# Expert tiles: remainders of at most 64 rows share a tile in pairs

## The chip, the cores and the metric

The kernel runs on one core of a Trainium2 chip. The metric is the device time in microseconds of one execution, the median of several runs. Engines are named as in the profile: PE (TensorE; PEld its weight loads), DVE (VectorE), ACT (ScalarE), POOL (GpSimd), SP (SyncE, whose queue the profile calls SPq).

## The reference, cut to what matters

2048 tokens (16 x 128) of 256 channels pass an attention-like step made of causal convolutions, and then a mixture of 16 experts with 4 choices a token, beside a shared expert.

```python
x = x + xattn(layernorm(x), k, bias, ctx, ctx)     # convolutions by head, products, sums over 8
xt = layernorm(x).reshape(-1, 256)                 # 2048 tokens
scores = softmax(xt @ Wg.T)                        # 16 experts in 4 groups
# the two best groups, in them the four best experts; their scores are the weights
h = silu(xt @ W1[e].T) * (xt @ W3[e].T)            # 176 wide, for each expert e
y = sum over the 4 choices of weight * (h @ W2[e].T)
z = silu(xt @ Ws1.T) * (xt @ Ws3.T) @ Ws2.T        # shared, 352 wide
x = x + y + z
```

## The kernel before, in words

The tokens are 16 units of 128. A first stage runs unit by unit: the convolutions as products with Toeplitz matrices, VectorE's products, and `sums` (line 1111), which adds them up by products with a 128x32 matrix whose outputs go to 32 partitions each, at 0, 32, 64 and 96 of one bank. From unit 6 on routing runs beside it on VectorE, four units at a time (`less_max` to `slots`).

GpSimd scatters each normalised row four times into `rows_scratch`, a region for each expert (line 563), together with its weights and its place in the output. The rows of an expert stand there in the order of the units. All experts' weights, 352 + 176 KB for each, are loaded once and stay in SBUF (`load_expert`, lines 263 to 269).

Then the shared expert runs on TensorE: `up_shared` (twelve steps), with `down_shared` for the unit outputs between. VectorE multiplies (`hidden_shared`), adds (`add_z`) and in between makes the tile lists: `tile_starts`, `tile_places`, `tile_owners`, `tile_ends` work on 128x256 arrays (a partition for each tile, an element for each unit and expert) and find each tile's expert, its first row and how many units it must wait for. TensorE turns these columns into rows in `tile_lists` (line 1217), in its order right behind step 9 of `up_shared`, with a wait on `owners_ready`. `last_sends` works out how many sends each read-back must await. `tile_map` writes the lists and signals `map_ready`; then SyncE gathers the first tiles.

The routed stage runs over 79 tiles of 128 rows (80, of which the last can't be needed), ordered by the unit in which a tile's first row lies. An expert with a remainder has one tile that is partly padding; tiles past the last real one work on padding. For each tile, in `routed_step` of each engine:
- SyncE: `gather` (lines 310 to 318) reads the tile's number from SBUF, waits until the tile four before was turned and taken, and starts a load of 144 KB.
- TensorE: `up` (line 1189), two products of 352 columns, then `turn_x` of the next tile (line 1208), `down` of the tile two before (line 1251), `turn_h` (line 1199). A float32 product shows as two records.
- ScalarE: silu, a copy of the turned rows, a copy of the output. VectorE: `take` (the two gate columns, line 955, behind a load of the expert's number), `hidden`, `copy_h`, `place` (the row numbers).
- GpSimd: `send`, an indirect DMA that writes 128 output rows to `y_scratch` (line 617).

When all tiles with rows of a pair of units have been sent, SyncE reads their 4 x 256 outputs back (`read_back`, 1 MB, after four loads of counts from SBUF, lines 322 to 328), VectorE adds them in four steps (`add_part`) and SyncE stores the units (`store`, line 332). In each turn of eight tiles one read-back and one store stand between the gathers; the last two units are read back one by one between the last gathers.

SyncE works in order: what waits in its queue holds all gathers behind it. The order on every engine is written out by hand; `routed` runs the first eight tiles unrolled, the others in a loop of four.

## Time and profile before

| | us |
|---|---|
| median of three runs | 414.01 (413.64 to 414.26) |
| the profiled execution | 410.32 |
| its span, first to last instruction | 408.6 |
| TensorE busy | 395.1 |
| VectorE, ScalarE, GpSimd busy | 241.7, 168.0, 185.1 |
| DMA, mean over the span | 195 GB/s |

The profile is of one execution. Busy times are sums over the span; matmuls are pipelined, so the record of one (its latency) is longer than its distance to the next, and distances between starts are what counts. The first stage ends at about 135 us, the shared expert's products run until 205, between them and the routed tiles at first; the first tile's up product is at 199.66. In a timeline a row gives the start, the length, the engine, the line, the operation with output and inputs, and how many instructions were put together.

### The profile page before, as it was taken

The numbers are of one execution on the slowest core, as the hardware profiler recorded it, in microseconds if no ns is written. First come the engines' busy times: TensorE is split into PE (matmuls) and PEld (weight loads), VectorE is DVE, ScalarE is ACT, GpSimd is POOL, SyncE is SP. The second block draws the span as 40 slices with busy tenths as digits, with TensorE's granted clock in tenths as the row PEclk, the third lists the DMA queues.
The fourth block names the chain that finished last, engine by engine and source line by source line (L and its number), as shares of the span: only waits on it lengthen the run. The fifth ranks groups of instructions, "written<-read, shape, count | busy, mean of one in ns | idle before, by whom it ended". The sixth has DMA issues, their size and how long they took to land.

```text
span 408.6 us, 9369 instructions
## 1 busy us (share of the span) xinstructions
PE 395.1 (97%) x2144; PEld 292.9 (72%) x2145; DVE 241.7 (59%) x663; ACT 168.0 (41%) x513; POOL 185.1 (45%) x231
## 2 busy tenths in 40 slices
PE   7999999999999999999999999999999999999994
PEld 6788788788888445555877777777676767677772
DVE  3576577898978447674344444464646464646464
ACT  5348557555653640111234334333343433333341
POOL 3253333338887644646463333333333333333344
PEclk9999999999999999999999999999999999999999
DMA  7964664468869996454443333646364645454662
GB/s 238 368 232 144 204 223 143 144 243 295 283 222 379 322 315 203 147 217 154 141 148 117 110 110 109 200 134 211 124 213 134 201 146 189 158 192 154 219 222 98
DMA packets 39421, 79.71 MB, mean 195 GB/s; under 512 B 5792, under 2 KB 26624, under 8 KB 37344
## 3 DMA queue, kind: packets, MB, share of 16 engines
q1 hardware_dynamic: 32528, 59.57, 44.5%
q0 software_dynamic: 6864, 19.80, 12.5%
q8 instruction: 12, 0.20, 0.2%
q14 instruction: 17, 0.14, 0.1%
HBM read 54.95 MB, written 24.40 MB: 194 GB/s over the span
## 4 chain that ended last, share of the span: by engine, by line
PE 69%; DVE 8%; DMA 7%; SPq 5%; issue 5%; POOL 3%; ACT 1%; DVEq 1%; POOLq 0%
PE heads L1189 17%; PE bank L1251 13%; PE heads L1097 9%; PE heads L1229 8%; PE bank L1241 5%; DMA toep<-rows_scratch 4%; PE heads L1099 4%; PE bank L1208 4%; DVE kv L636 3%; PE heads L1199 3%; PE bank L1111 3%; SPq L324 2%; DVE prod L665 2%; POOL rows_scratch L563 2%; DMA toep<-toep_in 2%
## 5 line engine op out<-in xcount | busy, mean ns | idle before, releaser
L617 POOL DMA_INDIRECT y_scratch<-toep,dest_i x79 | 76.6, 969 | 119.0 <-DVE dest_i L962 106.0
L1189 PE MATMUL heads<-w,toep 128*128 x316 | 106.6, 460 | 0.0
L1251 PE MATMUL bank<-w,toep 88*128 x316 | 82.0, 381 | 0.5 <-DVE toep L932 0.5
L563 POOL DMA_INDIRECT rows_scratch<-rows,slot_i x64 | 63.4, 991 | 38.9 <-issue 19.1
L1097 PE MATMUL heads<-toep,kv 128*128 128x256 f32 x256 | 77.8, 386 | 2.4 <-DVE kv L636 1.7
L1189 PEld LDWEIGHTS heads<-w,toep 128*128 128x128 f32 x316 | 53.8, 190 | 17.0
L458 ACT ACTIVATE toep<-heads 128x176 f32<-128x176 f32 x79 | 25.0, 317 | 82.9 <-PE heads L1189 82.9
L1251 PEld LDWEIGHTS bank<-w,toep 88*128 88x128 f32 x316 | 53.7, 190 | 6.1 <-issue 1.2
L932 DVE COPY toep<-heads 88x256 f32<-88x256 f32 x79 | 33.2, 421 | 37.9 <-PE heads L1199 37.8
L1099 PEld LDWEIGHTS heads<-toep,kv 128*128 128x128 f32 x256 | 48.6, 190 | 6.6
L665 DVE TENSOR_TENSOR prod<-heads,ctx_rep 128x1024 f32<-128x1024 f32 x32 | 39.0, 1219 | 22.2 <-PE bank L1111 19.8
L1099 PE MATMUL heads<-toep,kv 128*128 128x128 f32 x256 | 49.2, 274 | 0.0
L925 DVE SCALAR_TENSOR_TENSOR toep<-toep,heads 128x176 f32<-128x176 f32 x79 | 31.4, 397 | 27.4 <-ACT toep L458 24.6
L464 ACT ACTIVATE toep<-bank 128x256 f32<-128x256 f32 x79 | 30.3, 383 | 41.5 <-PE bank L1251 41.5
L1229 PE MATMUL heads<-xn_tr_all,ws 128*128 128x512 f32 (+1 forms) x96 | 43.1, 595 | 0.0
L1097 PEld LDWEIGHTS heads<-toep,kv 128*128 128x128 f32 x256 | 38.8, 192 | 3.2 <-DVE kv L636 1.8
L1208 PEld LDWEIGHTS bank<-ident,toep 128*128 128x128 f32 x158 | 21.9, 141 | 23.6 <-issue 11.0
L636 DVE TENSOR_TENSOR kv<-bank,ctx_tr 128x2048 f32<-128x2048 f32 x15 | 34.2, 2281 | 0.1
L452 ACT ACTIVATE toep<-bank 128x256 f32<-128x256 f32 x79 | 30.2, 382 | 5.7 <-PE bank L1208 5.6
L1208 PE MATMUL bank<-ident,toep 128*128 128x128 f32 x158 | 30.4, 274 | 1.6 <-DMA toep<-rows_scratch 1.6
L1229 PEld LDWEIGHTS heads<-xn_tr_all,ws 128*128 128x128 f32 (+1 forms) x96 | 16.9, 181 | 19.6 <-issue 19.3
L955 DVE COPY toep<-toep 128x2 f32 x79 | 14.0, 177 | 28.1 <-issue 22.3
(158 smaller groups left out, 439.8 us busy)
## 6 DMA issues: line engine op xcount, KB each, us to landing
ctx_rep<-ctxr_in SPq DMA_DIRECT2D x16, 1024.0 KB, 4.9
toep<-rows_scratch SPq DMA_DIRECT2D x79, 144.0 KB
prod<-y_scratch SPq DMA_DIRECT2D x7, 1024.0 KB, 5.2
w<-w_in SPq DMA_DIRECT2D x16, 352.0 KB
w<-w_in SPq DMA_DIRECT2D x16, 176.0 KB
rows_scratch<-pad_row SPq DMA_DIRECT2D x17, 144.0 KB
ctx_tr<-ctxt_in SPq DMA_DIRECT2D x16, 128.0 KB, 5.0
toep<-toep_in SPq DMA_DIRECT2D x4, 512.0 KB, 7.1
```

Of the source, the lines that this page charges most:

```text
L563: pool.indirect_dma_start(rows_d, bass.IndirectOffsetOnAxis(ap=slot_i[:, u, k:k + 1].bitcast(U32), axis=0), rows[:, u, :], None).then_inc( ...
L617: pool.indirect_dma_start(y_d, bass.IndirectOffsetOnAxis(ap=dest_i[b][:, 0:1].bitcast(U32), axis=0), y_sb[b], None).then_inc(y_sent[b], 16)
L636: nc.vector.tensor_tensor(kv[:, u % 2, :, :].rearrange("p b (g i j) -> p (b g) i j", i=C, j=C), tr_ps.rearrange("p b (g i) -> p (b g) i", ...
L665: nc.vector.tensor_tensor(prod[:, par, :, :], y_ps[par], ctx_rep[:, u % 2, par::2, :], ALU.mult).then_inc(prod_ready, 1)
L925: nc.vector.scalar_tensor_tensor(hid[p], act1[p], picked[:, b, 0:1], up_ps[p][:, INTER:], ALU.mult, ALU.mult).then_inc(hid_ready, 1)
L932: nc.vector.tensor_copy(hid_tr[p], ht_ps[p]).then_inc(htr_ready, 1)
L1097: nc.tensor.matmul(y_ps[par][:, i, :], kv[:, q, 0, h * P:(h + 1) * P], toep[:, q * HH + h, :], start=True, stop=False)
L1099: last = nc.tensor.matmul(y_ps[par][:, i, P:], kv[:, q, 1, h * P:(h + 1) * P], toep[:, q * HH + h, 0:P], start=False, stop=True)
L1189: last = nc.tensor.matmul(up_ps[p], x_tr[p][:, blk, :], w13[:, bass.ds(e, 1), blk, :].rearrange("p a n -> p (a n)"), start=blk == 0, stop= ...
L1208: last = nc.tensor.transpose(xt_ps[p][:, blk, :], src[:, blk * P:(blk + 1) * P], ident[:])
L1229: last = nc.tensor.matmul(bank[2 * (s % 2) + w][0:rows_c, :].rearrange("p (u n) -> p u n", u=GT), ws13[:, blk, w, c0:c0 + rows_c], xn_tr_a ...
L1251: last = nc.tensor.matmul(dn_ps[p], hid_tr[p][:, c, :], w2[:, bass.ds(e, 1), c, :].rearrange("p a n -> p (a n)"), start=c == 0, stop=c == 1)
```

## The change

The remainder of an expert that has at most 64 rows no longer gets a tile of its own. Such remainders are paired: two experts' share a tile, one in the rows 0 to 63, one in 64 to 127. There are 72 tiles, 64 + 8, and all are run. The tiles 16 to 23 are the mixed ones: they are gathered in two halves, their up and down products are two for each block, 64 columns of the stationary side each, into the partitions 0 to 63 and 64 to 127. The weights for the upper half are not indexed in SBUF: each mixed tile has its own 352 + 176 KB loaded from memory again (`load_other`), into buffers that are free by then, one pair of loads behind each of the gathers 8 to 15. Where fewer than eight pairs exist, a mixed tile works for one expert in both halves.

VectorE's lists grow by the columns for the second halves. `hidden_shared(5)`, `(8)` and `(9)` stand elsewhere among them. In the loop SyncE's four count loads of a read-back are put behind one gather each, the read-back and the store come together behind the fourth gather, and begin one turn later; the last four read-backs (two pairs and two single units) stand behind the last gather.

```diff
-TILES = TOK * TOPK // P + E
+TILES = TOK * TOPK // P + E // 2
+MIXED0, MIXED = 16, E // 2
+HALF = P // 2
...
-LIVE = TILES - 1
+LIVE = TILES
...
+        other_w13 = [mem[:, 0:W13].rearrange("p (b n) -> p b n", b=LB) for mem in other_mem]
+        other_w2 = [mem[0:HI, W13:W13 + W2].rearrange("p (c n) -> p c n", c=2) for mem in other_mem]
...
+            with eng.Fori(until // DEPTH, LIVE // DEPTH - 1) as it:
...
-                sp.dma_start(xg[b], rows_d[bass.ds(at, P)]).then_inc(rows_in[b], 16)
+                if is_mixed(t):
+                    sp.dma_start(xg[b][0:HALF], rows_d[bass.ds(at, HALF)]).then_inc(rows_in[b], 16)
+                    also = sp.value_load(other_row[0:1, t - MIXED0:t - MIXED0 + 1], min_val=0, max_val=E * REGION + HALF)
+                    sp.dma_start(xg[b][HALF:P], rows_d[bass.ds(also, HALF)]).then_inc(others_in[b], 16)
+                else:
+                    sp.dma_start(xg[b], rows_d[bass.ds(at, P)]).then_inc(rows_in[b], 16)
+            def load_other(g):
+                if g < 4:
+                    sp.wait_ge(s_up, GROUPS * len(CHUNKS))
+                elif g < 7:
+                    sp.wait_ge(s_down, UNITS)
+                e = sp.value_load(other_e[0:1, g:g + 1], min_val=0, max_val=E - 1)
+                sp.dma_start(other_w13[g].rearrange("p b n -> p (b n)"),
+                             w13_d[:, bass.ds(e, 1), :, :].rearrange("p a b n -> p (a b n)")).then_inc(other_in[g], 16)
+                sp.dma_start(other_w2[g].rearrange("p c n -> p (c n)"),
+                             w2_d[:, bass.ds(e, 1), :, :].rearrange("p a b n -> p (a b n)")).then_inc(other_in[g], 16)
...
+            for g in range(MIXED):
+                gathers(1, g, g + 1)
+                load_other(g)
+            gathers(2, 0, 8)
+            gathers(3, 0, 8)
+            for b in range(DEPTH):
+                gathers(4, b, b + 1)
             read_back(0, 0, 2, back, back_in)
-            gathers(3, 3, 8)
-            with sp.Fori(4, 9) as m:
-                gathers(m, 0, 2)
-                store(m - 4, m * 2 - 8, 2)
-                gathers(m, 2, 3)
-                read_back(m - 3, m * 2 - 6, 2, back, back_in)
-                gathers(m, 3, 8)
-            gathers(9, 0, 2)
-            store(5, 10, 2)
-            gathers(9, 2, 3)
-            read_back(6, 12, 2, back, back_in)
-            gathers(9, 3, 5)
-            read_back(7, 14, 1, back_last[0], last_in[0])
-            gathers(9, 5, 7)
-            read_back(8, 15, 1, back_last[1], last_in[1])
-            store(6, 12, 2)
-            store(7, 14, 1)
-            store(8, 15, 1)
+            gathers(4, 4, 8)
+            with sp.Fori(5, 9) as m:
+                sends = []
+                for b in range(DEPTH):
+                    gathers(m, b, b + 1)
+                    sends.append(sends_of(m - 4, b))
+                store(m - 5, m * 2 - 10, 2)
+                read_back(m - 4, m * 2 - 8, 2, back, back_in, sends)
+                gathers(m, 4, 8)
+            for i in range(4):
+                read_back(5 + i, SPANS[5 + i][0], SPANS[5 + i][1], back_last[i], last_in[i])
+                if i == 0:
+                    store(4, 8, 2)
+            for i in range(4):
+                store(5 + i, SPANS[5 + i][0], SPANS[5 + i][1])
...
+                all_rows = upto[:, :, UNITS - 1:UNITS].to_broadcast([P, E, UNITS])
+                then(nc.vector.scalar_tensor_tensor(short, first, -1.0 * HALF, all_rows, ALU.add, ALU.is_ge))
+                then(nc.vector.tensor_tensor(alone, in_units(short), starts, ALU.mult))
+                then(nc.vector.tensor_tensor(starts, starts, alone, ALU.subtract))
...
+                nc.vector.tensor_tensor_scan(one_row(place_of), go_on[:, 1:2].to_broadcast([P, UE]), one_row(starts), -1.0,
+                                             ALU.mult, ALU.add)
+                then(nc.vector.tensor_tensor_scan(one_row(alone_of), go_on[:, 1:2].to_broadcast([P, UE]), one_row(alone), 0.0,
+                                                  ALU.mult, ALU.add))
+            def mixed_places():
+                then(nc.vector.tensor_scalar(enough, io_2e[:], alone_of[:, UNITS - 1, E - 1:E], None, ALU.is_lt))
+                then(nc.vector.tensor_reduce(blocks_of, enough, AX_X, ALU.add))
+                nc.vector.tensor_scalar(mixed, io_p[:], MIXED0 - 0.5, None, ALU.is_gt)
+                then(nc.vector.scalar_tensor_tensor(late, io_p[:], -1.0 * MIXED0, blocks_of, ALU.add, ALU.is_ge))
+                nc.vector.scalar_tensor_tensor(mine, late, blocks_of, io_p[:], ALU.mult, ALU.subtract)
+                then(nc.vector.tensor_tensor(mixed, mixed, late, ALU.subtract))
+                then(nc.vector.scalar_tensor_tensor(mine, mixed, 1024.0, mine, ALU.mult, ALU.subtract))
+                then(nc.vector.tensor_scalar(sole, io_p[:], 2.0, 1.0 - 2 * MIXED0, ALU.mult, ALU.add))
+                then(nc.vector.tensor_scalar(own[7], sole, 1.0, None, ALU.add))
...
+                then(nc.vector.scalar_tensor_tensor(owns, place_of, mine, starts, ALU.is_equal, ALU.mult))
+                nc.vector.scalar_tensor_tensor(t0, alone_of, sole, alone, ALU.is_equal, ALU.mult)
+                then(nc.vector.scalar_tensor_tensor(t1, alone_of, own[7], alone, ALU.is_equal, ALU.mult))
+                nc.vector.tensor_reduce(own[2], one_row(t1), AX_X, ALU.add)
+                nc.vector.tensor_tensor(owns_other, owns, t1, ALU.add)
+                then(nc.vector.tensor_tensor(owns, owns, t0, ALU.add))
+                every = io_e[:].unsqueeze(1).to_broadcast([P, UNITS, E])
+                for i, who in enumerate((owns, owns_other)):
+                    nc.vector.tensor_tensor(t0 if i == 0 else t2, who, every, ALU.mult)
+                    last = nc.vector.scalar_tensor_tensor(t1 if i == 0 else t3, in_units(first), -1.0 * (P + E * REGION), who,
+                                                          ALU.add, ALU.mult)
+                    then(last)
+                nc.vector.tensor_reduce(own[0], one_row(t0), AX_X, ALU.add)
+                nc.vector.tensor_reduce(own[1], one_row(t1), AX_X, ALU.add)
+                nc.vector.tensor_reduce(own[3], one_row(t2), AX_X, ALU.add)
+                nc.vector.tensor_reduce(own[4], one_row(t3), AX_X, ALU.add)
+                nc.vector.tensor_reduce(own[5], one_row(owns), AX_X, ALU.add)
+                then(nc.vector.tensor_reduce(own[6], one_row(owns_other), AX_X, ALU.add))
...
+            def tile_lists_of():
+                past_full = float(TOK * TOPK // P)
+                then(nc.vector.tensor_scalar(dead_e, io_p[:], past_full - 0.5, None, ALU.is_gt))
+                nc.vector.tensor_scalar(own[7], io_p[:], past_full + E - 1, None, ALU.subtract)
+                nc.vector.tensor_scalar(lists[0], own[5], -1.0, 1.0, ALU.mult, ALU.add)
+                then(nc.vector.tensor_scalar(lists[3], own[6], -1.0, 1.0, ALU.mult, ALU.add))
+                then(nc.vector.tensor_tensor(dead_e, dead_e, own[7], ALU.mult))
+                then(nc.vector.tensor_scalar(dead_e, dead_e, E - 1.0, None, ALU.add))
+                nc.vector.scalar_tensor_tensor(lists[0], lists[0], dead_e, own[0], ALU.mult, ALU.add)
+                nc.vector.scalar_tensor_tensor(lists[3], lists[3], dead_e, own[3], ALU.mult, ALU.add)
+                nc.vector.scalar_tensor_tensor(lists[1], own[0], float(REGION), own[1], ALU.mult, ALU.add)
+                nc.vector.scalar_tensor_tensor(lists[4], own[3], float(REGION), own[4], ALU.mult, ALU.add)
                 nc.vector.tensor_scalar(of_expert, io_e[:], own[0], None, ALU.is_equal)
-                nc.vector.scalar_tensor_tensor(own[3], own[2], 0.0, own[0], ALU.max, ALU.add)
-                nc.vector.tensor_scalar(own[6], own[1], float(P + E * REGION), None, ALU.add)
-                then(nc.vector.scalar_tensor_tensor(own[4], own[0], float(REGION), own[1], ALU.mult, ALU.add))
+                nc.vector.tensor_scalar(own[7], own[2], -1.0 * HALF, float(HALF), ALU.mult, ALU.add)
+                then(nc.vector.tensor_scalar(own[6], own[1], float(P + E * REGION), None, ALU.add))
...
+                then(nc.vector.tensor_tensor(lists[4], lists[4], own[7], ALU.add))
...
+                    nc.vector.tensor_copy(full_to[:, at:at + 1], place_of[0:1, u0 + units - 1, E - 1:E])
+                    last = nc.vector.tensor_copy(alone_to[:, at:at + 1], alone_of[0:1, u0 + units - 1, E - 1:E])
                 then(last)
+                then(nc.vector.tensor_scalar(past, full_to, MIXED0 - 0.5, None, ALU.is_gt))
+                then(nc.vector.scalar_tensor_tensor(need, past, blocks_of[0:1], full_to, ALU.mult, ALU.add))
+                then(nc.vector.tensor_scalar(past, alone_to, 0.5, None, ALU.is_gt))
+                then(nc.vector.tensor_scalar(alone_to, blocks_of[0:1].to_broadcast([1, len(SPANS)]), MIXED0 - 1.0, None, ALU.add))
+                then(nc.vector.tensor_tensor(past, past, alone_to, ALU.mult))
+                then(nc.vector.tensor_tensor(need, need, past, ALU.max))
...
+                if is_mixed(t):
+                    dve.wait_ge(others_in[b], (t - MIXED0) // DEPTH * 16 + 16)
+                    nc.vector.tensor_copy(picked[0:HALF, b, :].unsqueeze(2), gates[0:HALF, :, bass.ds(e, 1)])
+                    e = dve.value_load(other_e[0:1, t - MIXED0:t - MIXED0 + 1], min_val=0, max_val=E - 1)
+                    nc.vector.tensor_copy(picked[HALF:P, b, :].unsqueeze(2), gates[HALF:P, :, bass.ds(e, 1)]).then_inc(taken, 1)
+                else:
+                    nc.vector.tensor_copy(picked[:, b, :].unsqueeze(2), gates[:, :, bass.ds(e, 1)]).then_inc(taken, 1)
...
             marks(3)
+            hidden_shared(5)
             places(3)
-            hidden_shared(5)
...
             tile_places()
+            mixed_places()
+            hidden_shared(8)
             tile_owners()
-            hidden_shared(8)
+            tile_lists_of()
             tile_ends()
+            hidden_shared(9)
             last_sends()
-            hidden_shared(9)
             tile_map()
...
+            for m in range(4):
                 steps(m, 0, 8)
-            steps(3, 0, 8, 0, 0)
-            with dve.Fori(4, 9) as m:
-                steps(m, 0, 8, m - 3, m * 2 - 6)
-            steps(9, 0, 6, 6, 12)
-            add_last(0, (0, 1))
-            steps(9, 6, 7)
-            add_last(0, (2, 3))
+            with dve.Fori(4, 8) as m:
+                steps(m, 0, 8, m - 4, m * 2 - 8)
+            steps(8, 0, 8, 4, 8)
             copy_h(LIVE - 1, (LIVE - 1) % 2)
-            add_last(1, range(TOPK))
+            for i in range(4):
+                add_last(i)
...
+                if is_mixed(t):
+                    g = t - MIXED0
+                    pe.wait_ge(other_in[g], 32)
+                    for blk in range(LB):
+                        nc.tensor.matmul(up_ps[p][0:HALF], x_tr[p][:, blk, 0:HALF],
+                                         w13[:, bass.ds(e, 1), blk, :].rearrange("p a n -> p (a n)"),
+                                         start=blk == 0, stop=blk == LB - 1)
+                        last = nc.tensor.matmul(up_ps[p][HALF:P], x_tr[p][:, blk, HALF:P], other_w13[g][:, blk, :],
+                                                start=blk == 0, stop=blk == LB - 1)
+                    last.then_inc(up_done, 1)
+                    return
...
+                for i in range(5):
+                    last = nc.tensor.transpose(map_ps[i], tmp[0:TILES, 8 + i:9 + i], ident[0:TILES, 0:TILES])
...
+                if is_mixed(t):
+                    for c in range(2):
+                        nc.tensor.matmul(dn_ps[p][0:HALF], hid_tr[p][:, c, 0:HALF],
+                                         w2[:, bass.ds(e, 1), c, :].rearrange("p a n -> p (a n)"),
+                                         start=c == 0, stop=c == 1)
+                        last = nc.tensor.matmul(dn_ps[p][HALF:P], hid_tr[p][:, c, HALF:P], other_w2[t - MIXED0][:, c, :],
+                                                start=c == 0, stop=c == 1)
+                    last.then_inc(dn_done, 1)
+                    return
...
```

## Rows read from the trace of the kernel before

**Rows 1.** The page, busy time of the engines over the span.

```profile
PE 395.1 (97%) x2144; PEld 292.9 (72%) x2145; DVE 241.7 (59%) x663; ACT 168.0 (41%) x513; POOL 185.1 (45%) x231
```

**Rows 2.** Chain that ended last, 185 to 408 us: by line; start, length, what.

```profile
by line: PE heads L1189 31.5%; PE bank L1251 24.1%; DMA toep<-rows_scratch 8.1%; PE bank L1208 6.7%; PE heads L1199 6.1%; PE bank L1241 4.7%; issue 4.4%; SPq L324 3.6%; PE heads L1229 3.1%; SPq L314 2.3%; SPq L318 1.1%; SPq L328 0.8%; DVEq 
...
392.16 0.87 PE bank L1251 x4
393.25 1.19 PE heads L1189 x4
```

**Rows 3.** Timeline of TensorE, routed stage: start, length, engine, line, operation.

```profile
205.28 1.35 PE L1189 MATMUL heads<-w,toep 128*128 x4
...
207.77 1.35 PE L1189 MATMUL heads<-w,toep 128*128 x4
...
398.06 1.35 PE L1189 MATMUL heads<-w,toep 128*128 x4
```

**Rows 4.** Chain that ended last, 272 to 290 us, around a read-back.

```profile
280.71 0.38 SPq L328
...
282.35 4.60 DMA toep<-rows_scratch
```

**Rows 5.** Timeline of TensorE, around the sums of one unit.

```profile
18.38 0.38 PE L1099 MATMUL heads<-toep,kv 128*128 128x128 f32 x2
18.70 1.07 PE L1111 MATMUL bank<-prod,sum_i 128*32 128x256 f32 x16
19.70 0.70 PE L1122 MATMUL bank<-vc,skip_w 128*128 128x256 f32 x2
20.23 0.38 PE L1077 MATMUL bank<-ident,v 128*128 128x128 f32 x2
```

**Rows 6.** Timeline of VectorE and TensorE, 175 to 190 us.

```profile
178.20 0.68 DVE L838 TENSOR_TENSOR_SCAN kv<-go_on,kv 128x256 f32<-128x256 f32 x1
...
181.06 0.15 DVE L850 SCALAR_TENSOR_TENSOR route_tmp<-io_p,kv 128x1 f32<-128x1 f32 x1
...
184.12 0.15 DVE L864 TENSOR_SCALAR route_tmp<-route_tmp 128x1 f32<-128x1 f32 x1
...
184.53 0.37 PE L1217 MATMUL bank<-ident,route_tmp 80*1 80x80 f32 x3
```

**Rows 7.** Start of TensorE; windows of the end: length, busy, clock, DMA, GB/s.

```profile
1.87 4.95 PE L1160 MATMUL heads<-ident 128*128 128x128 f32 x22 [1.87 <-POOL ident L521]
...
7.40 1.28 PE L1163 MATMUL heads<-ident 128*128 128x128 f32 x10
...
406.40:407.40 1.00, 0.00 (x0) 0.70 0.32 131
```

**Rows 8.** SyncE issuing expert weights; a window of the same stretch.

```profile
128.59 0.35 SPq L265 DMA_DIRECT2D w<-w_in  x1
...
129.91 0.35 SPq L265 DMA_DIRECT2D w<-w_in  x1
...
125.00:130.00 5.00, 4.53 (x40) 3.52 (x38) 3.31 (x7) 2.41 (x9) 4.17 (x5) 1.00 1.03 363
```

**Rows 9.** Last issues; a send; DMA landings (count, KB, median us); last addition.

```profile
389.84 1.49 SPq L318 DMA_DIRECT2D toep<-rows_scratch  x2
...
394.18 0.35 SPq L328 DMA_DIRECT2D ctx_rep<-y_scratch  x1
...
396.77 0.96 POOL L617 DMA_INDIRECT y_scratch<-toep,dest_i  x1 [1.33 <-DVE dest_i L962]
...
y_scratch<-toep,dest_i POOLq DMA_INDIRECT x79, 2.4
...
ctx_rep<-y_scratch SPq DMA_DIRECT2D x2, 512.0 KB, 3.6
...
out<-resid SPq DMA_DIRECT2D x2, 128.0 KB, 1.7
...
403.30 0.42 DVE L1037 TENSOR_TENSOR resid<-resid,ctx_rep 128x256 f32<-128x256 f32 x1
```

102 lines of the change are left out of this document (55 added, 47 removed).

## The prediction

> **What bounds the kernel now.** I read the page's busy shares first: TensorE is busy 97% of the span [rows 1], so only what lies on TensorE, or what makes it wait, can move the time. Then I read the chain that ended last, restricted to the stretch after 185 us: up to the last tile it is the up and down products, one after the other, with a small share for gathers and SyncE [rows 2]. One tile costs 1.19 us for the up product and 0.87 us for the down product; with its two pairs of transposes the pitch is 2.49 us (205.28 to 207.77), and from the up product of tile 2 to that of tile 78 it is 192.78 us for 76 tiles [rows 3]. 76 x 2.49 = 189.24, so about 3.5 us of the routed stage are waits. The chain names their kind: a read-back is issued at 280.71, behind the loads of its four counts, the next gather only at 282.35, and that gather takes 4.60 us to land behind the read-back's megabyte [rows 4]. After the last up product (398.06) the span runs on for 10.5 us.
>
> The span of this profile is 408.6 us, the profiled execution took 410.32 us, and the median of the runs is 414.01 us. I work out a difference on the span and add it to the median.
>
> **Seven tiles fewer.** 79 to 72 tiles at 2.49 us: -17.4 us. This is certain, since the count is static.
>
> **Eight mixed tiles.** Each does its up and down product twice, with 64 rows of output each. One after the other that would add 1.19 + 0.87 = 2.06 us a tile. The trace has a near relation: the sums of line 1111, which write 32 partitions each, at four different places of one bank. Sixteen records of 256 columns start at 18.70 and the next product at 19.70 [rows 5]. Two ordinary records of the same width take 0.53 us (19.70 to 20.23), or 0.43 where nothing switches, 0.21 each; 16 in a row would be 3.4 us. So products into different column groups run beside each other: 16 records in about four slots (0.85 us). Two groups of 64 should then run two at a time, and the eight records of a mixed up product take four slots, as the four of an ordinary one. What is left is the price of the change of shape. The last of the two ordinary records before the sums (18.38, 128 columns, 0.11 us each) is through at 18.60, the sums begin at 18.70, last 1.00 where four slots are 0.85, and the product behind takes 0.1 more than usual: some 0.36 us for each section [rows 5]. Part of it may be a wait that also exists without a switch, so I take 0.3. Sixteen sections: +4.8 us; bounds 0 and 8 x 2.06 = 16.5 us.
>
> The Trainium skill ("TensorE: Matmul & The Clock Gate", Measured speedup vs the span model) gives 2.38 times for three column tiles, 0.79 of the ideal. As an estimate from that page, two would give 1.59 times; on the durations above that is 0.31 + 0.23 us more a tile, 4.3 us for eight, and the whole would come out 0.5 us lower. The row of this trace has 3.4 times for four tiles. No row here shows two.
>
> **The tile lists on VectorE.** TensorE turns the lists (line 1217) at 184.53, right behind an up product of the shared experts; VectorE's last operation of the lists began at 184.12 [rows 6]. There is no room in this: what VectorE does longer ahead of it, TensorE waits. From the first scan at 178.20 to 181.06 are six operations of 128x256, 0.48 us each (0.45 without the longer scan); a small one is 0.15 long [rows 6]. The changed code has, between the same two points, 20 wide operations for 8, and 18 small ones more. 12 x 0.45 + 18 x 0.15 = 8.1 us. The three wide ones added to tile_starts fall into VectorE's waits there. Placing hidden_shared(5) ahead of places(3) puts 0.7 us of VectorE work behind a wait for ScalarE, and the shared down products wait for it: +0.75 us. hidden_shared(8), now in front of tile_owners, must first wait some 0.9 us for its silu. Less the half of that which the old wait cost already, and with two more list transposes (0.14), the lists are turned about 9.2 us later: +9.2 us, of which 8.4 is one wait of TensorE. Bounds 7 and 11. What is behind it (last_sends with 15 small operations more, some 2.3 us, map_ready and the first gather) is covered: TensorE still has two shared up products and five shared down products ahead of the first tile. If that cover were gone, those 2.3 us would count too.
>
> **The clock after this wait.** After TensorE's last product (through at 403.6) the granted clock is 1.00 until past 406.4 and averages 0.70 in the microsecond from there, half after it [rows 7]: it fell from 2.4 to 1.2 GHz about 3.3 us after the last work. A wait of 8.4 us is long enough. At the start, 22 transposes take 4.95 us and ten later ones 1.28, half the pace [rows 7] (the granted clock is shown as 1.00 there, the pace isn't). If work after the wait is as slow for 4.9 us, half of it is lost: +2.5 us; bounds 0 and 3.4.
>
> **The second experts' weights.** Eight loads of 528 KB, between the gathers of tiles 8 to 15. A pair of such loads holds SyncE for 1.32 us (128.59 to 129.91, a loop's branch in it; the issues alone are 0.35 each) [rows 8], the load of the expert's number some 0.65 (a quarter of the loads between 391.33 and 394.18, less the issue), the gather itself 1.15 (two in 1.49 us) [rows 9]. That is 2.8 to 3.1 us for a tile in 2.49, so SyncE falls 2.5 to 5 us behind over the eight. A gather is released when the tile four before is taken and used three pitches (7.5 us) later; the issue takes 1.3, the landing 2 to 3 (128 KB land in 1.7, rows 9), which leaves 3 to 4 us. So at the upper end some 2 us come through. Traffic would be 528 + 144 + 128 KB in 2.49 us, 320 GB/s, where the stretch 125 to 130 moved 363 [rows 8]. I take 1.0 us; bounds 0 and 6. The mixed tiles' second gather and VectorE's second load of an expert's number fit in the pitch.
>
> **Counts spread.** In the loop the four count loads (2.5 us) no longer stand between two gathers, five read-backs with stores become four: -3.3 of the 3.5 us; bounds 0 and -3.5.
>
> **The tail.** Let U be the start of the last up product. Before, the end is U + 10.5. Now four read-backs stand behind the last gather, each with its four loads in one row. The last gather's issue ended at 391.33 (U - 6.7) and the next read-back began 2.85 us later [rows 9]. Without a read-back ahead the last gather ends at about U - 7.2. Read-back of pair 5: U - 4.3. The store of pair 4 waits for VectorE: until U - 2.9. Then four loads, and a wait for the send of tile 67, the last with real rows (worked out from the counts per expert of the reference's inputs: 64 full tiles and four mixed hold all rows). A send starts 8.7 us after its up product (396.77 for tile 74, whose up product is at 398.06 - 4 x 2.49 = 388.1) and lands 3.4 later (its 0.96 and the 2.4 to the landing): U - 10.0 + 12.1 = U + 2.1. So read-backs at U + 2.2, 5.4, 8.6; the last lands 3.6 later, U + 12.2; four additions of 0.42, a store of 1.7, the end [rows 9]: U + 15.9. +5.4 us; bounds 2 and 7.
>
> **Sum.** -17.4 + 4.8 + 9.2 + 2.5 + 1.0 - 3.3 + 5.4 = +2.2 us: span 410.8, profiled execution 412.5, median 416.2 us. A difference below 0.8 us (0.2%) can't be told from none.
>
> **Rivals.**
> - *The change of shape costs nothing* (faster): the 0.36 us around the sums could be their semaphores or the one exposed load of weights. Place: 16 sections of the mixed tiles; -4.8 us, so -2.6, 411.4 us. It decides from below 0.16 us a section (0.3 less 2.2/16). For it: the sums do wait for products; against: the gap is the same at both ends of the sums.
> - *The clock doesn't fall, or recovers at once*: -2.5, so -0.3, 413.7 us. Against it stands the fall at the end of the trace.
> - *Gathers late behind the weights*: SyncE 5 us behind against 3 of slack (2 us), and each gather landing 2 us later behind the weights, as the one in rows 4 did behind its megabyte (2 us), where 1.0 is in the sum: +3, with sends that land late in the same traffic +4, 420.2 us. Against it: the weights are half a megabyte, and SyncE's issue of the gather gives them over a microsecond of lead.
> - *The halves run one after the other*: 16.5 for 4.8 us, 427.9 us. Against: rows 5. This is also the case in which the change does not do what it says.
>
> **How the numbers follow.** Forecast as worked out 0.46 (its own range 413 to 419); no cost of shape 0.22; clock 0.10; late gathers 0.14; one after the other 0.08. The range for 8 in 10 takes in the faster rival's centre and the late gathers: 410.4 to 420.8. Slower: late gathers and serial halves whole (0.22), and 0.35 of the forecast's 0.46: 0.57. Same: 0.08 of the forecast, 0.06 of the clock's rival, 0.03 of the first rival: 0.17. Faster: the rest, 0.26.
>
> **What would show it.** Lists: TensorE idle 8 us ahead of the list transposes, released by VectorE. Clock: a granted clock of 0.5 right behind. Mixed tiles: eight records of the up product in little over 1.2 us, pitch 3.1 us for eight tiles. Loads: no TensorE wait for gathers in tiles 8 to 24. Read-backs: pitch 2.49 throughout tiles 32 to 71. Tail: SyncE's loads in the chain, 16 us from the last up product to the end. I am wrong if the wait for the lists is under 5 us, or the mixed pitch is 2.5 or over 4.

## The result and the profile after

The changed kernel takes 423.11 us (median, 422.63 to 425.64) beside 414.13 for the kernel before in the same runs: ratio 1.0226, 95% interval 1.0187 to 1.0265. It is slower by 9.0 us, and its median lies above the upper end of the predicted range (420.8 us). On another chip, where the kernel before takes 409.9, the changed one took 421.59: ratio 1.0289 (1.0259 to 1.032). The profile before (410.32 us) is from an execution as fast as on that other chip, so the spans, 408.6 and 421.1, are compared by their 12.5 us. Why the kernel before takes some 4 us more in the runs beside the changed one than in its profile isn't shown: no profile of a 414 us execution is at hand.

The profile's page: TensorE is busy 386.0 us of 421.1, where it was 395.1 of 408.6 [rows 1], and the granted clock has a dip just before the middle (the slice from 189.5 to 200.0 us).

```profile
PE 386.0 (92%) x2126; PEld 276.9 (66%) x2127; DVE 246.9 (59%) x693; ACT 162.2 (39%) x492; POOL 179.2 (43%) x225
...
PEclk9999999999999999995999999999999999999996
```

The starts of the up products cut the span into parts, each against its counterpart:

| | forecast | measured | from |
|---|---|---|---|
| seven tiles fewer | -17.4 | -17.4 | 7 x 2.49 |
| tile lists turned later | +9.2 | +10.0 | 184.53 to 194.50 |
| clock behind it | +2.5 | +2.4 | lists to first up product: 15.13, now 17.58 |
| mixed tiles | +4.8 | +4.7 | pitches of tiles 16 to 25 over 2.49 |
| late gathers, tiles 10 to 15 | +1.0 | +3.0 | pitches over 2.49 |
| read-backs in the loop | -3.3 | +3.1 | loss 3.5 before, 6.6 now |
| tail | +5.4 | +6.7 | last up product to the end: 10.54, now 17.25 |
| sum | +2.2 | +12.5 | |

**Lists and clock.** TensorE's timeline around the lists; the last two rows are windows (length, busy time, granted clock, DMA share, GB/s). The up product ends the work, the transposes of the lists come 8.33 us later, and the shared products behind them are slow. For the wait the profile names no releaser (`<-issue`). That it is VectorE is read from the program, in which the transposes wait for `owners_ready`, and from the times: VectorE's last list operation ends at 194.44, the transposes start at 194.50. Of the products behind them 12 records of 256 columns take 4.90 us here and 2.80 in the kernel before. The clock averages 0.70 over 7.9 us, that is 4.7 us at 1.2 GHz, half of it (2.4 us) lost.

```profile
179.14 7.03 PE L1350 MATMUL heads<-xn_tr_all,ws 128*96 128x512 f32 x16
194.50 0.76 PE L1338 MATMUL bank<-ident,route_tmp 72*1 72x72 f32 x5 [8.33 <-issue]
195.05 4.90 PE L1362 MATMUL bank<-ws,ctx_rep 128*128 128x256 f32 x12
199.79 3.60 PE L1350 MATMUL heads<-xn_tr_all,ws 128*128 128x512 f32 x8
```

```profile
194.50:202.40 7.90, 7.90 (x24) 0.70 0.25 79
202.40:206.50 4.10, 4.10 (x11) 1.00 0.51 149
```

VectorE in the same stretch: from hidden_shared(8) to the last operation of the lists it works without a wait, 11.0 us.

```profile
183.46 0.68 DVE L1045 TENSOR_TENSOR ctx_rep<-kv,heads 96x512 f32<-96x512 f32 x1 [0.82 <-ACT kv L521]
184.06 0.47 DVE L915 SCALAR_TENSOR_TENSOR kv<-kv,route_tmp 128x256 f32<-128x256 f32 x1
...
194.29 0.15 DVE L959 TENSOR_SCALAR route_tmp<-route_tmp 128x1 f32<-128x1 f32 x1
```

**Mixed tiles.** One record of each half starts in each slot (lines 1300 and 1303), slots 0.29 us apart but for the first, 0.35; the tile's pitch is 3.07 (264.41 to 267.48). Against an ordinary tile the extra lies at the changes of shape: 0.13 us ahead of the up product (0.35 from the transposes to it, where 0.22 is usual), and some 0.15 each behind it, ahead of the down product and behind that.

```profile
264.41 0.51 PE L1300 MATMUL heads<-w,toep 128*64 x1
264.42 0.51 PE L1303 MATMUL heads<-ws,toep 128*64 128x352 f32 x1
264.76 0.46 PE L1300 MATMUL heads<-w,toep 128*64 x1
264.76 0.46 PE L1303 MATMUL heads<-ws,toep 128*64 128x352 f32 x1
...
267.48 0.51 PE L1300 MATMUL heads<-w,toep 128*64 x1
```

The weight loads (PEld) show a difference at just these places. At a change the load starts with its product (264.41 and 264.41; 265.74 and 265.75), while within ordinary tiles it starts 0.11 us or more ahead (316.77 for the product at 316.88). That this makes the price fits its size (a load is 0.13 to 0.14 long), but no run tested it.

```profile
264.41 0.13 PEld L1300 LDWEIGHTS heads<-w,toep 128*64 128x64 f32 x1 [0.18 <-issue]
...
316.77 0.89 PEld L1308 LDWEIGHTS heads<-w,toep 128*128 128x128 f32 x4
```

**Loads of weights.** With the two loads between them SyncE issues its gathers 3.2 us apart (seven such distances from 227.70 to 250.08), against a pitch of 2.49, so it falls 5.0 us behind. Then a gather is late: turn_x comes 0.37 us after the up product of tile 12 is through (242.69 + 1.19), and the next up product after 3.03 us instead of 2.49.

```profile
242.69 1.35 PE L1308 MATMUL heads<-w,toep 128*128 x4
244.25 0.44 PE L1329 MATMUL bank<-ident,toep 128*128 128x128 f32 x2 [0.21 <-DMA toep<-rows_scratch]
...
245.72 1.35 PE L1308 MATMUL heads<-w,toep 128*128 x4
```

**Read-backs.** Three engines at one of them: SyncE starts the read-back at 387.72; VectorE's first addition, next in its order, has waited 1.94 us for the megabyte when it starts at 392.81; behind it in VectorE's order stand `take`, `hidden` and `copy_h` of the next tile, and the down product (395.07) waited 0.82 us for that copy. The last row sums such waits over 275 to 395 us (us, times, longest). The same question to the kernel before gives no row: there VectorE never waited for a read-back between 275 and 395 us.

```profile
387.72 0.01 SPq L376 DMA_DIRECT2D prod<-y_scratch  x1
```

```profile
392.81 0.69 DVE L1141 TENSOR_TENSOR prod<-prod 128x512 f32<-128x512 f32 x1 [1.94 <-DMA prod<-y_scratch]
```

```profile
395.07 1.13 PE L1381 MATMUL bank<-w,toep 88*128 x4 [0.82 <-DVE toep L1037]
```

```profile
DVE prod L1141 <- DMA prod<-y_scratch: 9.2, 5, 2.3
```

In the kernel before the first addition stands 5.98 us behind the issue of its read-back (280.71 in rows 4, the addition below, without a wait), at the others 5.5 to 5.8, and a read-back takes 5.0 to 5.3 us to land, as the second row says (least, median, most). So there was at most a microsecond of room. In the changed kernel VectorE was ready for its addition at 390.87, only 3.15 us behind the issue at 387.72: the read-back comes some 2.5 us later against VectorE's order.

```profile
286.69 0.69 DVE L1029 TENSOR_TENSOR prod<-prod 128x512 f32<-128x512 f32 x1
```

```profile
DMA to landing us min/median/max: 5.0/5.2/5.3
```

**Tail.** The last up product starts at 403.85 = U. SyncE's read-backs: 407.08 (U + 3.2), 409.84, and the last of the two in the row at 412.5 (U + 8.7); each gap (2.8 and 2.7 us) is four count loads, though the chain of the profile puts the last 0.3 us of them down to a send that landed at 412.48. VectorE then waits for the last one and adds.

```profile
407.08 0.37 SPq L376 DMA_DIRECT2D ctx_rep<-y_scratch  x1
409.84 3.03 SPq L376 DMA_DIRECT2D xn_tr_all<-y_scratch  x2
```

```profile
417.31 0.42 DVE L1141 TENSOR_TENSOR xn_tr_all<-xn_tr_all 128x256 f32<-128x256 f32 x1 [0.68 <-DMA xn_tr_all<-y_scratch]
...
418.56 0.43 DVE L1149 TENSOR_TENSOR resid<-resid,xn_tr_all 128x256 f32<-128x256 f32 x1
```

### The profile page after: what moved, and what is told of

It reads as the page before. It is cut to its first block, busy times and chain, and to the rows that moved or that the text cites. A ratio compares the mean times of both kernels' runs of the same rounds, so it can differ in the third digit from the quotient of the medians.

```text
span 421.1 us, 9096 instructions
## 1 busy us (share of the span) xinstructions
PE 386.0 (92%) x2126; PEld 276.9 (66%) x2127; DVE 246.9 (59%) x693; ACT 162.2 (39%) x492; POOL 179.2 (43%) x225
## 3 DMA queue, kind: packets, MB, share of 16 engines
q0 software_dynamic: 6528, 18.88, 11.6%
## 4 chain that ended last, share of the span: by engine, by line
PE 56%; DVE 12%; issue 10%; DMA 10%; SPq 8%; DVEq 2%; another core or an unknown queue 1%; ACT 1%; POOL 0%; POOLq 0%; ACTq 0%
PE heads L1205 10%; PE heads L1308 8%; PE bank L1381 7%; DMA prod<-y_scratch 6%; PE heads L1350 6%; PE bank L1362 6%; PE heads L1207 5%; DVE kv L684 3%; PE bank L1219 3%; PE heads L1300 2%; PE heads L1318 2%; PE bank L1329 2%; DVE prod L713 2%; SPq L340 2%; PE bank L1373 2%
## 5 line engine op out<-in xcount | busy, mean ns | idle before, releaser
L667 POOL DMA_INDIRECT y_scratch<-toep,dest_i x72 | 71.0, 986 | 133.9 <-DVE dest_i L1072 116.4
L1308 PE MATMUL heads<-w,toep 128*128 x256 | 86.7, 461 | 0.7 <-issue 0.4
L1381 PE MATMUL bank<-w,toep 88*128 x256 | 66.8, 384 | 3.6 <-DVE toep L1037 3.5
L1308 PEld LDWEIGHTS heads<-w,toep 128*128 128x128 f32 x256 | 43.6, 190 | 15.5 <-issue 1.7
L1037 DVE COPY toep<-heads 88x256 f32<-88x256 f32 x72 | 30.2, 420 | 35.4 <-PE heads L1318 35.3
L1381 PEld LDWEIGHTS bank<-w,toep 88*128 88x128 f32 x256 | 43.6, 190 | 9.3 <-issue 5.0
L513 ACT ACTIVATE toep<-bank 128x256 f32<-128x256 f32 x72 | 27.7, 384 | 45.6 <-PE bank L1381 23.2
L1030 DVE SCALAR_TENSOR_TENSOR toep<-toep,heads 128x176 f32<-128x176 f32 x72 | 28.6, 397 | 24.2 <-DVE toep L1067 9.0
L1329 PEld LDWEIGHTS bank<-ident,toep 128*128 128x128 f32 x144 | 19.4, 141 | 23.6 <-issue 13.5
L1318 PE MATMUL heads<-ident,toep 128*88 128x128 f32 x144 | 27.9, 275 | 2.0 <-DVE toep L1030 2.0
L501 ACT ACTIVATE toep<-bank 128x256 f32<-128x256 f32 x72 | 27.6, 383 | 5.6 <-PE bank L1329 5.4
```

Source lines behind the costliest of these rows:

```text
L667: pool.indirect_dma_start(y_d, bass.IndirectOffsetOnAxis(ap=dest_i[b][:, 0:1].bitcast(U32), axis=0), y_sb[b], None).then_inc(y_sent[b], 16)
L1037: nc.vector.tensor_copy(hid_tr[p], ht_ps[p]).then_inc(htr_ready, 1)
L1308: last = nc.tensor.matmul(up_ps[p], x_tr[p][:, blk, :], w13[:, bass.ds(e, 1), blk, :].rearrange("p a n -> p (a n)"), start=blk == 0, stop= ...
L1318: last = nc.tensor.transpose(ht_ps[p][:, c, :], hid[p][:, c * HI:(c + 1) * HI], ident[:])
L1329: last = nc.tensor.transpose(xt_ps[p][:, blk, :], src[:, blk * P:(blk + 1) * P], ident[:])
L1381: last = nc.tensor.matmul(dn_ps[p], hid_tr[p][:, c, :], w2[:, bass.ds(e, 1), c, :].rearrange("p a n -> p (a n)"), start=c == 0, stop=c == 1)
```

## The experiments

They ran on three chips. On the first the kernel before takes 414.77 us (lists later, TensorE kept busy, additions later, no loads), on the second 410.10 (new order alone, read-back earlier, halves, first try), on the third 409.92 (the changed kernel again, loads spread in the kernel before, second try). The changed kernel wasn't run on the first two, so gains over its median (423.11, or 421.59 on the third) are differences between occasions, good to some 2 us; the traces carry the argument. Spans are from their profiles; the changed kernel's is 421.1, and 418.7 when it was run again.

**Lists turned later on TensorE.**

```diff
                 if last_up:
                     up_shared(s)
+                    tile_lists()
...
-                if s == 9:
-                    tile_lists()
...
             hidden_shared(9)
-            last_sends()
-            tile_map()
             add_z(8)
             add_z(9)
+            last_sends()
+            tile_map()
```

> The changed kernel, with the turning of the tile lists on TensorE moved behind step 11 of up_shared, and add_z(8), add_z(9) on VectorE ahead of last_sends. Theory: the 8.3 us in which TensorE waits for VectorE's lists, and the half clock behind it (2.4 us), are the 12.4 us by which the first up product came later. With 9.5 us of shared products in the place of the wait, the first up product comes at 203 to 206 instead of 212 us, with the clock at 1.00, and the kernel is 6 to 9 us faster than the changed one (median 414 to 417). Rival (the front is bounded by map_ready and the gathers, not by TensorE's order): the wait only moves to map_ready, and the first up product stays later than 209 us.

417.98 us, ratio to the kernel before 1.0072 (1.0039 to 1.0105), against 1.0226 for the changed one. The first up product is at 207.0 instead of 212.1. So the wait was a cost that the order on TensorE can avoid, but the gain of 5.1 us stayed under the forecast of 6 to 9: up_shared(11) needs hidden_shared(9), which VectorE does only after the lists. TensorE still waited 2.9 us, and the clock still fell (0.57 on average over the four microseconds from 195, in the second row).

```profile
195.43 5.17 PE L1350 MATMUL heads<-xn_tr_all,ws 128*96 128x512 f32 x8 [2.91 <-DVE kv L1045]
...
195.00:199.00 4.00, 3.58 (x5) 0.57 0.27 103
```

**TensorE kept busy in the wait.**

```diff
+                for _ in range(72):
+                    nc.tensor.transpose(bank[7][:, 0:P], ident[:], ident[:])
                 pe.wait_ge(owners_ready, 1)
```

> The changed kernel, with 72 transposes of the identity (7.7 us of work whose result nobody reads) between the waits of tile_lists, ahead of the one for VectorE's lists. Theory: the clock fell in the 8.3 us wait; kept busy, it stays at 1.00, the shared products behind it take 2.4 us less, and the median is 2 to 3 us below 423.1. Rival (the products behind the wait were slow for another reason, or the clock falls anyway): no change within 0.5 us.

420.58 us, ratio 1.0139 (1.0081 to 1.0196). In the trace the 12 records behind the lists take 2.81 us instead of 4.90, the clock is 1.00 throughout 188 to 204, and the first up product comes 1.5 us earlier although the lists were ready 0.8 us later in this run: from the transposes of the lists to it are 15.24 us, 17.58 in the changed kernel, 15.13 in the one before. The median is 2.5 us below 423.1, but the intervals of the two ratios overlap, so it is the trace that shows the clock's term. What TensorE still waited is put down to VectorE's last list operation here (line 959).

```profile
187.06 8.02 PE L1337 MATMUL bank<-ident 128*128 128x128 f32 x72
...
195.32 0.47 PE L1340 MATMUL bank<-ident,route_tmp 72*1 72x72 f32 x5 [0.24 <-DVE route_tmp L959]
195.63 2.81 PE L1364 MATMUL bank<-ws,ctx_rep 128*128 128x256 f32 x12
```

**Additions two tiles later.**

```diff
-                    if pair is not None and 1 <= j <= 4:
-                        add_pair(pair, u0, j - 1)
+                    if pair is not None and 3 <= j <= 6:
+                        add_pair(pair, u0, j - 3)
```

> The changed kernel, with VectorE's four additions of a read-back two tiles later (behind tiles 3 to 6 of a turn instead of 1 to 4). Theory: in the routed loop TensorE loses 6.6 us at five read-backs because VectorE, in order, waits 1.1 to 2.3 us for the read-back's megabyte and holds hidden and copy_h of the next tiles; two tiles later the megabyte is there and the loss goes down to under 1.5 us: 5 to 6 us faster than the changed kernel. Rival (the gathers behind the read-back land late, as before the change): the loss stays over 4 us, since nothing of SyncE's order changes.

420.37 us, ratio 1.0129 (1.0073 to 1.0185). The loss at the read-backs went from 6.6 to 1.0 us, with SyncE's order unchanged: it was VectorE's wait, not late gathers. Of these 5.6 us, 4.0 were given back in the tail, 21.3 us instead of 17.3. The last addition of pair 4 now stands in VectorE's order behind the copy of row numbers (`place`), which waits 2.44 us for a send to land (a send issued at 393.51, beside a read-back, took 6.82 us). SyncE's store of pair 4 waits for that addition, and the next read-backs stand behind this store; VectorE then stood 3.58 us for the next of them. The forecast of 5 to 6 us left this out; the median is 2.7 us lower.

```profile
404.75 0.69 DVE L1149 TENSOR_TENSOR resid<-resid,ctx_rep 128x512 f32<-128x512 f32 x1
409.02 0.69 DVE L1141 TENSOR_TENSOR ctx_rep<-ctx_rep 128x512 f32<-128x512 f32 x1 [3.58 <-DMA ctx_rep<-y_scratch]
```

**No loads of second experts' weights.**

```diff
                 gathers(1, g, g + 1)
-                load_other(g)
...
-                    pe.wait_ge(other_in[g], 32)
```

> The changed kernel without the eight loads of second experts' weights and without the wait for them; the upper halves of the mixed tiles use what lies in those buffers, so their outputs are not the reference's. Theory: the 2.9 us that TensorE loses at tiles 12 to 15 are gathers late behind these loads: the pitch there is 2.49 and the kernel 2.5 to 3 us faster than the changed one, while the mixed tiles keep their pitch of 3.07 (change of column groups). Rival (the mixed tiles' pitch comes from waits for gathers or weights): their pitch falls too, another 4 us.

421.66 us, ratio 1.0162 (1.0094 to 1.0229). The tiles up to 14 have the pitch 2.49 again, tile 15 has 2.59 (loss 0.1 in all instead of 3.0), 246.22 to 248.71 below, and the mixed tiles keep 3.07. The median gained 1.5 us, less than the trace's 3: this profile's first up product was at 213.2, 1.1 us later than in the changed kernel, for no reason that the edit gives.

```profile
246.22 1.35 PE L1306 MATMUL heads<-w,toep 128*128 x4
...
248.71 1.35 PE L1306 MATMUL heads<-w,toep 128*128 x4
```

**The kernel before with SyncE's new order alone.** Loads spread, and store and read-back behind the fourth gather; the first read-back, ahead of this loop, is also moved behind the fourth gather, with its four loads left together:

```diff
             with sp.Fori(4, 9) as m:
-                gathers(m, 0, 2)
-                store(m - 4, m * 2 - 8, 2)
-                gathers(m, 2, 3)
-                read_back(m - 3, m * 2 - 6, 2, back, back_in)
-                gathers(m, 3, 8)
+                sends = []
+                for b in range(DEPTH):
+                    gathers(m, b, b + 1)
+                    sends.append(sends_of(m - 3, b))
+                store(m - 4, m * 2 - 8, 2)
+                read_back(m - 3, m * 2 - 6, 2, back, back_in, sends)
+                gathers(m, 4, 8)
```

> The kernel before with one part of the change alone: in SyncE's loop the four count loads stand behind one gather each, and store and read-back together behind the fourth gather instead of in front of and behind the third. Theory: what costs is that the read-back is issued one gather later, while VectorE's additions stay where they were and wait in order for its megabyte; the loss of TensorE at the read-backs grows from 3.5 us to 5 to 7 us, and this kernel is 2 to 3 us slower than the kernel before. Rival (the loads between the gathers cost, and spread they are hidden): the loss falls below 1 us and the kernel is 2 to 3 us faster.

415.95 us beside 410.10, ratio 1.0162 (1.0123 to 1.0201); the profile's span is 412.4 and its loss at the read-backs 8.0 us. This is slower than the expected 2 to 3 us: 5.9 between the medians, 3.8 between the spans, since the profiled execution was the fastest of four (414.11 to 418.85). VectorE's waits for read-backs (275 to 395 us) appear in the old kernel too:

```profile
DVE prod L1035 <- DMA prod<-y_scratch: 8.6, 5, 2.0
```

**The kernel before with the loads spread and the read-back left behind the third gather.** The same edit with three gathers ahead of the read-back and the store behind the first.

> The kernel before with the count loads spread behind one gather each, but the read-back where it was, behind the third gather (the store behind the first). Theory: spread loads by themselves gain, and only the later read-back lost: TensorE's loss at the read-backs falls from 3.5 us to under 1, the kernel is 2 to 3 us faster than the kernel before. Rival (the loads between gathers slow the gathers themselves): no gain, or slower.

406.85 beside 409.92, ratio 0.9922 (0.9892 to 0.9951). The loss is 0.3 us and the last up product starts at 394.76 instead of 398.06 [rows 3]: 3.3 us, the size that the prediction gave to the spreading. Spreading gains 3 us; the place one gather later makes a loss of 8.0 out of 0.3. That place includes the store, which stood right ahead of the read-back in the run above (as in the changed kernel) and stands behind the first gather here: how much of the lateness is the gather and how much the store wasn't separated.

```profile
394.76 1.35 PE L1197 MATMUL heads<-w,toep 128*128 x4
```

**The changed kernel with the read-back one gather earlier.** The same edit there; the first read-back comes one gather earlier too, with its four loads left together.

> The changed kernel with the read-back one gather earlier (behind the third), three loads spread and the fourth right ahead of it, and the store behind the first gather. Theory: the megabyte lands 2 to 2.5 us earlier, so VectorE's wait for it (1.8 us each) goes, and the loss at read-backs falls from 6.6 to under 2 us: 4 to 5 us faster than the changed one (median 418 to 419). Rival (the loss is late gathers): no gain.

417.82 beside 410.10, ratio 1.0189 (1.0159 to 1.0218); span 416.1. This is 3.8 us below 421.59. The four read-backs of the loop cost nothing, the first one 2.8 us. That is the rival's kind of loss: behind the first read-back, issued at 298.51, a gather took 6.97 us to land and VectorE waited 3.34 us for a send. Its four loads in a row are a likely part of it, but not all: with these loads spread, in the second try below, 1.2 us are left, behind a send that took 6.44 us to land.

**The halves one after the other.**

```diff
                                          w13[:, bass.ds(e, 1), blk, :].rearrange("p a n -> p (a n)"),
                                          start=blk == 0, stop=blk == LB - 1)
+                    for blk in range(LB):
                         last = nc.tensor.matmul(up_ps[p][HALF:P], x_tr[p][:, blk, HALF:P], other_w13[g][:, blk, :],
                                                 start=blk == 0, stop=blk == LB - 1)
...
+                    for c in range(2):
                         last = nc.tensor.matmul(dn_ps[p][HALF:P], hid_tr[p][:, c, HALF:P], other_w2[t - MIXED0][:, c, :],
```

> The changed kernel with the products of a mixed tile in another order: both blocks of the lower half, then both of the upper one, instead of in turns. In turns, the records of the two halves start within 0.01 us of each other, four slots of 0.29 us for an up product. If only neighbouring products into different column groups run together, the order lower, lower, upper, upper leaves one such pair in the middle: six slots for eight records, 0.6 us more for the up and 0.4 for the down product, pitch of a mixed tile 4.0 instead of 3.07, 8 us more in all. If TensorE picks from further down its queue, nothing changes (3.07).

421.64 (two executions) beside 410.10 and span 418.9, as the changed kernel when run again (421.59 and 418.7). The pitch of a mixed tile is 3.08. The four records of the lower half (line 1300) and the four of the upper (line 1304) stand behind each other in the program and still start in pairs:

```profile
268.84 0.51 PE L1300 MATMUL heads<-w,toep 128*64 x1
268.85 0.51 PE L1304 MATMUL heads<-kv,toep 128*64 128x352 f32 x1
...
269.77 0.46 PE L1300 MATMUL heads<-w,toep 128*64 x1
269.79 0.46 PE L1304 MATMUL heads<-kv,toep 128*64 128x352 f32 x1
270.18 0.44 PE L1330 MATMUL bank<-ident,toep 128*128 128x128 f32 x2
```

**All parts mended, first try.** Lists late with hidden_shared(9) ahead of tile_lists_of, places(3) ahead of hidden_shared(5) again, early read-backs, and in the tail pair 5 read back behind gather 69, counts loaded ahead of the waits. The part in the lists:

```diff
             tile_owners()
+            hidden_shared(9)
             tile_lists_of()
             tile_ends()
-            hidden_shared(9)
+            add_z(8)
+            add_z(9)
             last_sends()
             tile_map()
```

> All that the runs point to, on the changed kernel: tile lists turned behind step 11 with hidden_shared(9) ahead of tile_lists_of, places(3) back ahead of hidden_shared(5), the read-back one gather earlier, and a new tail: pair 5 read back behind gather 69 and added within the last tiles, the counts of the last three read-backs loaded ahead of their waits. Expected by terms against the changed kernel (421.1 us span): front 8 us less (first up product at 204), read-backs 5 us less, tail 2 us less: span 406, median 408, which is 6 us faster than the kernel before. If the front only moves its wait to map_ready: 411.

410.02 beside 410.10, ratio 0.9984 (0.996 to 1.0009): no difference from the kernel before, where 6 us less were expected (11.6 us below 421.59, though). The first up product came at 204.2 as expected, but TensorE waited 3.1 us for add_z(10), which VectorE did only behind last_sends, and the clock fell once more; the first step took 4.3 us. Loads and first read-back kept their losses (3.3 and 1.9 us).

**Second try.** The first try with `last_sends` behind the map and the weights loaded earlier; the edit is against the changed kernel:

```diff
+            tile_map()
             hidden_shared(10)
             hidden_shared(11)
             add_z(10)
             add_z(11)
+            last_sends()
...
                 gather(t, t % DEPTH, t // DEPTH)
+                if t >= DEPTH:
+                    load_other(t - DEPTH)
...
                 gathers(1, g, g + 1)
-                load_other(g)
+                if g % 2:
+                    load_other(MIXED // 2 + g // 2)
```

> The version with all parts, mended where its trace showed waits: last_sends behind the map, so that the map comes 4 us sooner and hidden_shared(10) and (11) with it; four of the second experts' weights are loaded behind gathers 4 to 7, the others behind every second gather from 9 on; the counts of the first read-back are spread too. Expected by terms against the version before it (span 408.1): front 3 to 5 us less (first up product at 200 to 201, with the clock at full), loads 2 us less, first read-back 1.9 less: span 399 to 401, some 9 us faster than the kernel before on the same chip. If the clock falls in what is left of the wait, 2 us less of that.

403.74 beside 409.92, ratio 0.9849 (0.9825 to 0.9874), span 402.8: faster than both kernels, by 6.2 and by 17.9 us. The lists are turned right behind an up product, the clock stays at 1.00 (186 to 230 us), the first up product is at 200.25, the tail 15.0 us. The expectation was 399 to 401: tiles 5 to 7, where the weights are loaded now, lose 2.8 us, which was not followed further, the tiles from 9 to 15 lose another 0.6, the first read-back still costs 1.2 and one late tile 0.7.

```profile
187.06 7.03 PE L1375 MATMUL heads<-xn_tr_all,ws 128*128 128x512 f32 x16
193.93 0.48 PE L1363 MATMUL bank<-ident,route_tmp 72*1 72x72 f32 x5
194.24 2.81 PE L1387 MATMUL bank<-ws,ctx_rep 128*128 128x256 f32 x12
...
387.81 1.35 PE L1333 MATMUL heads<-w,toep 128*128 x4
```

**The changed kernel again.** No edit.

> The changed kernel itself, beside the kernel before on the chip of the next two runs. The kernel before measured 414 on two occasions and 410.1 on a third, and the profile shown of it took 410.3; the changed kernel took 423.1 beside 414.1. If the difference is the sum of the terms read from the two traces (12.5 us), it is 11 to 13 us on a chip where the kernel before takes 410, and 9 to 10 where it takes 414.

421.59 us beside 409.92: 11.7 us of difference, inside the expected 11 to 13.

## Why the prediction was wrong

The sign was right, the size wasn't: +2.2 forecast, +9.0 measured (+12.5 between the profiles). Four of the seven terms held within 0.8 us. One term was off by 6.4 us, more than the other misses together; with it as forecast the median would have been an estimated 416.7 (423.11 less 6.4), inside the range.

- **Tiles, mixed tiles.** -17.4 and +4.7 for 4.8. Two column groups of 64 run side by side, eight records in four slots, and what is left lies at the changes of shape: 0.29 us a section (4.7/16; a late gather of 0.2 at tile 16 is in it), where I took 0.3 from the sums [rows 5]. The estimate from the Trainium skill ("TensorE: Matmul & The Clock Gate", Measured speedup vs the span model: 2.38 times for three column tiles) would have given 4.3. By its size it isn't out, but it takes the loss for one of running side by side, and the rows above show two full column groups in each slot. Rivals one (no cost of shape) and four (one after the other) are out.
- **Lists.** +10.0 for 9.2. From the first scan to the last operation of the lists VectorE took 8.7 us more, against 8.1 for the operations and some 0.5 for hidden_shared(8). The first scan came 1.5 us later, where I had 0.75; 0.87 of it is TensorE's longer wait for the additions (1.38 for 0.51). That this is the swap of places(3) is shown by the second try, which undoes it: the scan is at 178.14 again, 178.20 in the kernel before. (The terms of this forecast as I named them add up to 9.4, not 9.2.) The place, the releaser and the sign of this term were right, and moving the lists and filling the wait showed it.
- **Clock.** +2.4 for 2.5; filling the wait gave 2.3 us of it back in the trace (15.24 for 17.58). Rival two (the clock doesn't fall) is out.
- **Loads.** +3.0 for 1.0. A gather with its loads took SyncE 3.2 us, where I had 2.8 to 3.1, so it fell 5.0 us behind, the upper end of what I gave, and more came through than the 1.0 I took. The run without the loads shows that all but 0.1 of it is theirs. It lies between the forecast and rival three, which had 3 us more.
- **Counts spread: the step that failed.** I wrote "five read-backs with stores become four: -3.3 of the 3.5 us". This priced the loads that stood between two gathers, and nothing else of the moved step. The read-back itself was moved behind one more gather, with the store ahead of it, some 2.5 us later against VectorE's additions, which stayed behind tiles 1 to 4 of a turn. In the kernel before the read-back issued at 280.71 [rows 4] was just in time for them (landed after some 5.2 us, wanted after 5.98); that cover was not looked at. VectorE waited 9.2 us at five of them, with the next tiles' hidden and copy_h behind, and TensorE lost 6.6 us there: +3.1 where I had -3.3. Shown both ways: additions later on VectorE (6.6 to 1.0), or the read-back back at its place (only the first still costs), and in the old kernel the order alone turns a gain of 3 us into a loss of 6. The forecast -3.3 is what spreading gives if the read-back stays where it was. Two of my signs answer the same way: the pitch was not 2.49 throughout tiles 32 to 71, and TensorE did wait for gathers in tiles 12 to 15.
- **Tail.** +6.7 for 5.4. The parts were as written: SyncE's loads in a row, the wait for the send of tile 67, the last read-back at U + 8.7 where I had U + 8.6. That this fits so well is luck: the first of the three came 1.0 us late, since the send took 4.5 us to land and not 3.4, and the two gaps were 1.0 us shorter together. The last read-back's landing took 4.6 us for 3.6; the read-back before it, issued 2.7 us earlier, may be the reason, which wasn't tested.

The range was too narrow for the same reason: its upper end was drawn by gathers behind the weights, and no case had a read-back that comes late for VectorE, though the bound of that term was given as 0 to -3.5, which excludes a loss without a reason.

## What to carry to other kernels

When a transfer is moved in one queue, find its consumer and ask when, in its engine's own order, it is wanted: a wait of an in-order engine that isn't the bottleneck still holds all that it owes to the one that is. A bound of "nothing to a gain" on a moved step needs a reason that excludes a loss. Bookkeeping on a side engine that is turned by the bottleneck engine should be given a place where that one has independent work to put in front, since the wait costs twice: once itself, and once through the clock behind it.

## What the runs showed of the hardware that was not expected

- TensorE starts products of different column groups in pairs even where four records of the one group stand ahead of the first of the other in the program (268.84/268.85 to 269.77/269.79): for two groups of 64 columns the order of the products didn't matter.
- The clock had fallen to 1.2 GHz behind a wait of 2.9 us in one run (0.57 on average in 195 to 199, lists later) and of 3.1 us in another (0.50 in 202 to 206, first try).
- Beside a read-back of a megabyte other transfers land late: a gather of 144 KB in 4.60 us (kernel before) and 6.97 (read-back earlier), sends in 5.16, 6.44 and 6.82 us, where 2.4 is the median.
- The same program differs from chip to chip or from one occasion to the next, which these runs don't tell apart: the kernel before took 409.9, 410.1 and 414.8 us on three chips, one occasion each, and 414.1 in the runs of the result; the changed kernel took 421.6 beside 409.9 and 423.1 beside 414.1. So 1% can come without any change of the kernel. Between the two kernels there were 11.7 and 9.0 us; the intervals of the ratios just touch (1.0259 and 1.0265), so whether this difference changes too is open.
